# Routed experts of a transformer block: token rows and expert hidden values turned on TensorE in two fp16 parts instead of one fp32 transpose

## What is computed

```
logits = flat @ router_w
scores = softmax(logits)
_, topk_idx = top_k(logits + router_bias, 4)
topk_scores = scores[topk_idx] / sum(scores[topk_idx])
g = silu(einsum('nd,edf->nef', flat, wg))        # 64 experts, d = 512, f = 128
u = einsum('nd,edf->nef', flat, wu)
routed = einsum('ne,nef,efd->nd', comb, g * u, wd)
shared = einsum('nsh,shd->nd', silu(flat@swg) * (flat@swu), swd)
out = x + routed + shared
```

## Time and profile before

| | us |
|---|---|
| three runs: median, lowest, highest | 1222.91, 1222.49, 1225.0 |
| the profiled execution, its own time | 1227.31 |
| its span, from the first to the last instruction | 1225.5 |

### The profile page before, as it was taken

The page is one execution under the profiler, slowest core; times in us unless marked ns, Lnnn a source line. Parts: engine busy times, 40 slices in busy tenths (PEclk is TensorE's granted clock), DMA queues, the critical chain, the costliest instruction groups (busy, mean ns, idle before and its releaser), DMA issues.

```text
span 1225.5 us, 27577 instructions
## 1 busy us (share of the span) xinstructions
PE 1129.8 (92%) x9096; PEld 513.7 (42%) x9097; DVE 732.4 (60%) x1134; ACT 501.2 (41%) x944; POOL 422.1 (34%) x548
## 2 busy tenths in 40 slices
PE   6957899999999998999998999999999999997998
PEld 3523233333333333554444455544545454532443
DVE  6755899999999983877794123323323222335383
ACT  3311588889888897235211122222222222201010
POOL 5400134343343434015636323322333322145460
PEclk9979699999999999999999999999999999998999
DMA  8143232232312200521000588779886888665461
GB/s 241 66 129 110 41 81 41 53 65 40 77 40 52 65 21 21 187 105 34 1 1 16 168 298 283 249 246 327 264 269 184 279 293 286 189 165 175 151 178 63
DMA packets 75766, 169.98 MB, mean 139 GB/s; under 512 B 13764, under 2 KB 16324, under 8 KB 75716
## 3 DMA queue, kind: packets, MB, share of 16 engines
q1 hardware_dynamic: 45972, 100.59, 27.3%
q0 software_dynamic: 12800, 41.95, 11.8%
q10 hardware_dynamic: 16944, 26.75, 6.3%
HBM read 225.08 MB, written 41.42 MB: 217 GB/s over the span
## 4 chain that ended last, share of the span: by engine, by line
PE 65%; DVE 14%; issue 8%; DMA 6%; ACT 4%; POOL 1%; SPq 1%; DVEq 0%; ACTq 0%; POOLq 0%
PE PS L1320 13%; PE PS L1211 12%; PE PS L1336 7%; PE PS L1128 6%; PE PS L1293 6%; DVE maxes L1394 5%; PE PS L1307 4%; PE PS L1015 4%; PE PS L1181 3%; DVE max_low L1394 3%; DMA ring<-in_L_ffn_wg_dram 3%; PE PS L1106 3%; PE PS L1077 3%; ACT att L902 2%; PE PS L1328 2%
## 5 line engine op out<-in xcount | busy, mean ns | idle before, releaser
L902 ACT ACTIVATE att<-PS 128x512 f32<-128x512 f32 x576 | 312.6, 594 | 58.6 <-PE PS L1106 51.7
L1211 PE MATMUL PS<-XN,att 128*128 128x512 f16 x768 | 177.5, 392 | 16.2 <-issue 8.0
L1128 PE MATMUL PS<-att,v_head 128*32 128x256 f32 (+1 forms) x2560 | 178.6, 370 | 0.9 <-POOL att L717 0.9
L1394 DVE TENSOR_REDUCE maxes<-PS 128x2 f32<-128x1024 f32 (+2 forms) x192 | 172.8, 941 | 1.2 <-PE PS L1020 1.1
L1394 DVE TENSOR_REDUCE max_low<-PS 128x2 f32<-128x1024 f32 x128 | 153.7, 1210 | 20.5 <-PE PS L1015 18.1
L1015 PE MATMUL PS<-att 48*128 48x512 f16 (+7 forms) x768 | 117.9, 332 | 19.8 <-DMA att<-k_stacks 13.5
L1684 DVE TENSOR_TENSOR w_att<-w_att,PS 128x128 f32<-128x128 f32 x96 | 27.6, 288 | 168.6 <-issue 86.9
L966 ACT ACTIVATE w_att<-PS 128x512 f32<-128x512 f32 x96 | 57.2, 597 | 172.5 <-PE PS L1307 172.5
L1696 DVE COPY w_att<-PS 128x512 f32<-128x512 f32 x96 | 66.4, 692 | 101.1 <-DMA slot_y<-w_att 71.2
L1211 PEld LDWEIGHTS PS<-XN,att 128*128 128x128 f16 x768 | 76.3, 100 | 115.3 <-issue 23.6
L1106 PE MATMUL PS<-att 50*128 50x512 f16 (+1 forms) x640 | 112.0, 363 | 13.5 <-ACT att L902 11.1
(11 more groups left out here) (169 smaller groups left out, 1371.6 us busy)
## 6 DMA issues: line engine op xcount, KB each, us to landing
ring<-in_L_ffn_wg_dram SPq DMA_DIRECT2D x96, 512.0 KB
XT<-in_L_ffn_wg_dram SPq DMA_DIRECT2D x96, 512.0 KB
ring<-in_L_ffn_wd_dram SPq DMA_DIRECT2D x96, 256.0 KB
XT<-in_L_ffn_wd_dram SPq DMA_DIRECT2D x96, 256.0 KB
slot_y<-w_att ACTq DMA_DIRECT2D x192, 128.0 KB
att<-q_stacks SPq DMA_DIRECT2D x64, 192.0 KB, 3.9
q_stacks<-att SPq DMA_DIRECT2D x24, 256.0 KB
att<-k_stacks SPq DMA_DIRECT2D x64, 96.0 KB, 4.0
```

Source lines behind the costliest of these rows:

```text
L902: act.activation(probs[:, n0 % RING, u * BANK:(u + 1) * BANK], bank((2 * n0 + u) % EXP_BANKS), ACT.Exp, scale=HD ** -0.5 / QK_SCALE ** 2). ...
L1128: mm = pe.matmul(PS[32 * r:32 * r + 32, at:at + qn], v_head[b][:, kt, :], probs[:, (NS * b + s) % RING, a:a + qn], start=s in (0, NS0), st ...
L1211: mm = pe.matmul(bank(2 * (n % 2) + k), shared_w[:, 2 * k + w, C * s + c, at:at + P], v[:, c, tokens], start=(c == 0 and w == 0 and v is x ...
L1394: last = dve.reduce_max(out, src, AXX)
```

## The change

It does five things.

1. `turn_slots` on PE: the four fp32 transposes of a pair's tokens become eight fp16 matmuls against an fp16 identity, `xg_hi` and `xg_lo` added up in PSUM. In place of the gather's semaphore it waits for `xg_lo_done`.
2. The two parts are made in the loop: `tokens_high` on ACT (`xg` times 16, rounded to fp16), and `tokens_low` on DVE (the rest). Both read `xg` with a step of four elements and write without one. In body n they stand for pair n+2: on ACT behind `silu(n)`, on DVE behind `hidden_turned(n-1)`. Those of pairs 0 and 1 stand ahead of the loop. The scale is taken out again in `turned_tokens`.
3. The same for the hidden values: `e_high(n)` on ACT, `e_low(n)` on DVE, and two fp16 matmuls in `turn_hidden` in place of one fp32 transpose, the scale of 32 taken out in `hidden_turned`.
4. Gathers leave empty places out: the table holds token - 2048 for a filled slot, 2048 is added as it is copied, so an empty slot has index 2048, which the bounds check of the indirect DMA leaves out. POOL clears `xg` once ahead of the first gather. The gathers wait for `xg_lo_done` instead of `xg_turned`.
5. POOL makes the fp16 identity near the start of the program.

The new tiles `ht_hi` and `ht_lo` take the free end of `w_att`, `xg_hi` and `xg_lo` a part of `XT` behind the weights of lanes 4 to 7. The diff, without the declarations of the tile `ident_h` and of six semaphores:

```diff
--- before.py
+++ after.py
@@ -52,6 +52,7 @@
 
 
 X_SCALE, W_SCALE = 16.0, 64.0
+H_SCALE = 32.0
 XW = X_SCALE * W_SCALE
 QK_SCALE = 16.0
 
@@ -318,6 +320,8 @@
         lane_w += [carve(flat_xt, n * 3 * C * F, [P, 3, C * F])[0] for n in range(4)]
         xg, xgt, yb, sg, ht, hg = carve_all(w_att, 0, ([P, 4, D], FP32), ([P, 2, D], FP32), ([P, 2, D], FP32),
                                             ([P, 2, P], FP32), ([P, 2, P], FP32), ([P, 2, P], FP32))
+        ht_hi, ht_lo = carve_all(w_att, 4 * D + 2 * D + 2 * D + 6 * P, ([P, 2, P], F16), ([P, 2, P], F16))
+        xg_hi, xg_lo = carve_all(flat_xt, 4 * 3 * C * F, *[([P, 2, D], F16)] * 2)
         idx = sb("idx", [P, 4], U32)
 
         hot = [carve_all(arena, at, ([P, NT, 2 * PAIRS], F16), ([P, NT, SUB], F16))
@@ -641,6 +651,8 @@
                 pool.tensor_tensor(parts[n][2], parts[n][0], parts[n][1], ALU.subtract).then_inc(att_w_lo, 1)
 
             part_scale(0)
+            pool.wait_ge(ident_set, 1)
+            pool.tensor_copy(ident_h[:, :], ident[:, :]).then_inc(ident_h_set, 1)
             for b in range(BATCH):
                 pool.memset(v_head[b][:, :, :], 1 / X_SCALE).then_inc(v_ones, 1)
             pool.memset(mask_q[:, :], 0.0).then_inc(mask_zero, 1)
@@ -760,7 +772,8 @@
                 .then_inc(consts, 1)
             pool.tensor_copy(iota_c[:, :], idxf[:, 0:4, :].rearrange("p a b -> p (a b)").bitcast(U32))\
                 .then_inc(consts, 1)
-            pool.tensor_copy(token_f[:, :], token_f[:, :].bitcast(U32)).then_inc(consts, 1)
+            pool.tensor_scalar(token_f[:, :], token_f[:, :].bitcast(U32), float(-NTOK), None, ALU.add)\
+                .then_inc(consts, 1)
             pool.tensor_copy(iota_t[:, :, :], iota_t[:, :, :].bitcast(U32)).then_inc(consts, 1)
             pool.wait_ge(consts, 15)
 
@@ -820,15 +833,18 @@
             def gather_tokens(i, j):
                 n = JP * i + j
 
-                wait(pool, xg_turned, n - 3)
+                wait(pool, xg_lo_done, n - 3)
                 pool.tensor_copy(idx[:, j:j + 1], tab_t[:, bass.ds(j * LANE_TILES + i, 1)]).then_inc(idx_set, 1)
                 wait_alone(pool, idx_set, n + 1, pool_passed)
                 pool.indirect_dma_start(out=xg[:, j, :], out_offset=None, in_=xn2_rows[:, :],
-                                        in_offset=bass.IndirectOffsetOnAxis(ap=idx[:, j:j + 1], axis=0))\
+                                        in_offset=bass.IndirectOffsetOnAxis(ap=idx[:, j:j + 1], axis=0),
+                                        bounds_check=NTOK - 1, oob_is_err=False)\
                     .then_inc(xg_in[j], 16)
 
             pool.wait_ge(table_ready, 1)
             pool.wait_ge(xn2_stored, 16 * NT)
+            pool.memset(xg[:, :, :].rearrange("p n d -> p (n d)"), 0.0).then_inc(xg_zero, 1)
+            pool.wait_ge(xg_zero, 1)
             for j in range(JP):
                 gather_tokens(0, j)
             with pool.Fori(1, LANE_TILES) as i:
@@ -959,16 +975,29 @@
             for g in range(EARLY):
                 shared_silu(g)
 
+            def tokens_high(n, k, i):
+
+                act.wait_ge(xg_in[k % JP], 16 * (i + k // JP + 1))
+                wait(act, xg_turned, n - 1)
+                act.activation(xg_hi[:, k % 2, :].rearrange("p (c k) -> p c k", c=C),
+                               xg[:, k % JP, :].rearrange("p (k c) -> p c k", c=C), ACT.Copy, scale=X_SCALE)\
+                   .then_inc(xg_hi_done, 1)
+
             def turned_tokens(n, k):
                 act.wait_ge(xg_turned, n + 1)
 
                 wait(act, e_up, n - 1)
-                act.activation(xgt[:, k % 2, :], bank(k % 2), ACT.Copy).then_inc(xgt_ready, 1)
+                act.activation(xgt[:, k % 2, :], bank(k % 2), ACT.Copy, scale=1 / X_SCALE).then_inc(xgt_ready, 1)
 
             def silu(n, k):
                 act.wait_ge(e_up, n + 1)
                 wait(act, e_hidden, n - 1)
                 act.activation(sg[:, k % 2, :], bank(2 + k % 2, F), ACT.Silu).then_inc(e_silu, 1)
+
+            def e_high(n, k):
+
+                act.wait_ge(e_hidden, n + 1)
+                act.activation(ht_hi[:, k % 2, :], ht[:, k % 2, :], ACT.Copy, scale=H_SCALE).then_inc(e_hidden_hi, 1)
 
             def store_y(i, j):
                 act.wait_ge(yb_ready, JP * i + j + 1)
@@ -983,9 +1012,14 @@
                     if not (last and j == JP - 1):
                         turned_tokens(n + 1, j + 1)
                     silu(n, j)
+                    if not (last and j >= JP - 2):
+                        tokens_high(n + 2, j + 2, i)
+                    e_high(n, j)
                     if not (first and j < 3):
                         store_y(i if j == 3 else i - 1, (j + 1) % JP if j < 3 else 0)
 
+            for k in range(2):
+                tokens_high(k, k, 0)
             turned_tokens(0, 0)
             expert_pairs(0, True, False)
             with act.Fori(1, LANE_TILES - 1) as i:
@@ -1298,14 +1332,15 @@
             for g in range(EARLY):
                 shared(g)
 
-            def turn_slots(n, k, i):
-                j = k % JP
-                pe.wait_ge(xg_in[j], 16 * (i + k // JP + 1))
+            def turn_slots(n, k):
+                pe.wait_ge(xg_lo_done, n + 1)
 
                 wait(pe, xgt_ready, n - 1)
                 for c in range(C):
-                    mm = pe.transpose(PS[:, (k % 2) * BANK + c * P:(k % 2) * BANK + (c + 1) * P],
-                                      xg[:, j, c:D:C], ident[:, :])
+                    at = slice((k % 2) * BANK + c * P, (k % 2) * BANK + (c + 1) * P)
+                    part = slice(c * P, (c + 1) * P)
+                    pe.matmul(PS[:, at], xg_hi[:, k % 2, part], ident_h[:, :], start=True, stop=False)
+                    mm = pe.matmul(PS[:, at], xg_lo[:, k % 2, part], ident_h[:, :], start=False, stop=True)
                 mm.then_inc(xg_turned, 1)
 
             def expert_up(n, j, i):
@@ -1323,9 +1358,10 @@
                 mm.then_inc(e_up, 1)
 
             def turn_hidden(n, j):
-                pe.wait_ge(e_hidden, n + 1)
+                pe.wait_ge(e_hidden_lo, n + 1)
                 wait(pe, e_turned, n - 1)
-                pe.transpose(bank(6 + j % 2, P), ht[:, j % 2, :], ident[:, :]).then_inc(e_turn, 1)
+                pe.matmul(bank(6 + j % 2, P), ht_hi[:, j % 2, :], ident_h[:, :], start=True, stop=False)
+                pe.matmul(bank(6 + j % 2, P), ht_lo[:, j % 2, :], ident_h[:, :], start=False, stop=True).then_inc(e_turn, 1)
 
             def expert_down(n, j, i):
                 for l in range(2):
@@ -1342,7 +1378,7 @@
                 for j in range(JP):
                     n = JP * i + j
                     if not (last and j == JP - 1):
-                        turn_slots(n + 1, j + 1, i)
+                        turn_slots(n + 1, j + 1)
                     expert_up(n, j, i)
                     if not (first and j < 1):
                         turn_hidden(n - 1, (j - 1) % JP)
@@ -1351,7 +1387,8 @@
 
 
             pe.wait_ge(table_ready, 1)
-            turn_slots(0, 0, 0)
+            pe.wait_ge(ident_h_set, 1)
+            turn_slots(0, 0)
             expert_pairs(0, True, False)
             with pe.Fori(1, LANE_TILES - 1) as i:
                 expert_pairs(i, False, False)
@@ -1670,7 +1707,7 @@
                         hidden_low(n - 1)
                     if n == TABLE_AT + 1:
                         dve.wait_ge(table_done, 1)
-                        dve.tensor_copy(tab_t[:, :], bank(6, PAIRS)).then_inc(table_ready, 1)
+                        dve.tensor_scalar(tab_t[:, :], bank(6, PAIRS), float(NTOK), None, ALU.add).then_inc(table_ready, 1)
                 if g:
                     hidden_low(HC * (g + 1) - 1)
                 for t in range(4 * g, 4 * g + 4) if g else ():
@@ -1683,11 +1720,23 @@
                 at = (2 + j % 2) * BANK + F
                 dve.tensor_tensor(ht[:, j % 2, :], sg[:, j % 2, :], PS[:, at:at + F], ALU.mult).then_inc(e_hidden, 1)
 
+            def tokens_low(n, k):
+                dve.wait_ge(xg_hi_done, n + 1)
+                dve.scalar_tensor_tensor(out=xg_lo[:, k % 2, :].rearrange("p (c k) -> p c k", c=C),
+                                         in0=xg[:, k % JP, :].rearrange("p (k c) -> p c k", c=C), scalar=X_SCALE,
+                                         in1=xg_hi[:, k % 2, :].rearrange("p (c k) -> p c k", c=C), op0=ALU.mult,
+                                         op1=ALU.subtract).then_inc(xg_lo_done, 1)
+
+            def e_low(n, j):
+                dve.wait_ge(e_hidden_hi, n + 1)
+                dve.scalar_tensor_tensor(out=ht_lo[:, j % 2, :], in0=ht[:, j % 2, :], scalar=H_SCALE,
+                                         in1=ht_hi[:, j % 2, :], op0=ALU.mult, op1=ALU.subtract).then_inc(e_hidden_lo, 1)
+
             def hidden_turned(n, j):
                 dve.wait_ge(e_turn, n + 1)
 
                 wait(dve, e_down, n - 1)
-                dve.tensor_copy(hg[:, j % 2, :], bank(6 + j % 2, P)).then_inc(e_turned, 1)
```

(6 more changed lines are left out.)

7 lines of the change are left out of this document (added).

## The result

| | before | changed |
|---|---|---|
| median of four runs, us | 1222.7 | 1324.3 |
| lowest to highest, us | 1222.42 to 1225.0 | 1315.83 to 1327.32 |
| span of the profiled execution, us | 1225.5 | 1321.7 |

The ratio is 1.083, with a 95% interval of 1.078 to 1.088: about 101 us slower, outside the range of 1230 to 1305.

A forecast was written before the change was run, and what follows sets the result against it. The prediction took PE alone to bound the loop most of the time, at 3.83 us a pair. Terms 25.9 + 2 + 0.3 + 0.56 = +28.7 us on 1227.3 gave 1256.0, or 1251.6 against the median; range 1230 to 1305.

The forecast's parts named there:

- The closed chain: Routed loop: silu, both token conversions, token turn and up product follow one another, 4.23 us a pair, +25.9 us; chance 0.60.
- Where I chose: the step of four: Token conversions on ACT and DVE: reading xg with a step of 16 bytes was taken to cost nothing extra.
- the double price on both engines: Token conversions: time per element doubles on ACT and DVE, 92 us more, 1344 us; chance 0.07, left out of the range.
- the 2 us kept for late weights: Routed loop: waits for weights that remain despite the longer beat, 2 us, between 0 and 5.
- The other reading of the same rows: Weight load with the step: 0.07 us more for 128 elements, as a price per element 0.28 us on each engine.
- doublings: Token conversions at doubled time per element: 0.45 us more on ACT alone (1294 us), or also 0.53 on DVE (1344).
- PE's beat without waits: Routed loop: fp16 turns take 0.23 and 0.15 us off PE's beat of 3.83, leaving 3.45 us.
- The rows left out: Gathers in the loop: 4096 rows, 8.4 MB or 8% of bytes, moving the time by a microsecond or two at most.
- PE's idle time: Routed loop, before the token turn: PE stands idle some 0.7 us in every pair, released by DVE.
- The second: Rival for the loop: same chain, but the step of four costs time, 1294 to 1344 us; chance 0.27.
- The third: Rival for the loop: conversions run early enough, PE never waits, beat 3.45 us, total 1197 us; chance 0.05.
- The fifth: Rival for the loop: PE's idling lowers its clock; at half, products take twice as long, far above range; chance 0.04.

The follow-up runs named there:

- e1: Changed kernel with both token conversions reading and writing without a step, PE's weight loads taking the step instead; ratio to the kernel before 1.019.
- e2: Changed kernel, step kept, with tokens_high moved ahead of silu and tokens_low ahead of the hidden product; ratio to the kernel before 1.041.
- e3: Changed kernel with both the step removed from the conversions and their place moved ahead of silu and the hidden product; ratio to the kernel before 0.989.
- e7: Kernel before plus ten instructions behind its last work, reading 512 fp32 elements at steps 1 to 8; step 4 took 1.10 us on ACT, 1.06 on DVE.
- e6: Kernel before with only the hidden values split and turned by two fp16 products; ratio to the kernel before 0.998.
- e9: Changed kernel with empty slots holding index 0 again, so all 12,288 rows are fetched; ratio to the kernel before 1.082.
- e4: Kernel before with only the gathers' part: empty places left out by the bounds check, xg cleared once; ratio to the kernel before 0.991.
- e8: Changed kernel with conversions reading without a step but writing fp16 elements 256 bytes apart; 1768 us in its one run.
- e10: e3 with yb stores issued ahead of e_high and tokens_low of pairs 0 and 1 ahead of the last two shared additions; ratio to the kernel before 0.982.
- e12: e10 with empty slots holding index 0, so all 12,288 rows are fetched again; ratio to the kernel before 0.988.

## Why the prediction was wrong

**The mechanism held.** The closed chain from up product to up product through silu, `tokens_high`, `tokens_low` and the token turn is in the trace, link by link, with PE's wait released by DVE 94 times. e1, which takes the step away and leaves the place, has 4.14 us a beat where the sum said 4.23. e2 and e3 show that the place is what makes the chain.

**The step that failed is "Where I chose: the step of four".** I took nothing for it and gave the double price on both engines a chance of 0.07 and no place in the range. Measured, it is 0.51 us on ACT and 0.37 on DVE. The rest of the beat nearly cancels: 0.10 more for the eight products (0.55 and not 0.45), 0.11 less since ACT starts `tokens_high` 0.17 us after silu's start and not after its end, and 0.10 less between engines (0.04 + 0.04 + 0.06 and not 0.07 + 0.07 + 0.10). 4.23 + 0.51 + 0.37 + 0.10 - 0.11 - 0.10 = 5.00, as measured. Without the step the same sum gives 4.12, and e1 has 4.14. Over 94 beats 0.77 us more are 72 us, and with the slow first bodies the loop came out 76.9 us above the forecast 397.6, nearly the whole distance from 1252 to 1324; the 2 us kept for late weights weren't needed.

**What misled** was the earlier trace rows. That four weight loads with the step stand 0.12 us apart was read as a property of SBUF that holds for every engine. It holds for PE's loads: contiguous ones stand 0.12 us apart too (eight of L1190 in 1.01 us). The other reading of the same rows, 0.07 us more for 128 elements, gives 0.28 per 512 and was too low as well: e7 has 0.47 and 0.38. Where the Trainium skill ("SBUF — State Buffer", in its part on the DMA port swizzle) states a penalty and no row of the trace covers the engine in question, the price should have stood in the middle of the range and not at its rim. And two "doublings" were set apart from each other as if one engine might pay and the other not; they read the same memory with the same step.

**Smaller terms.** PE's beat without waits was put at 3.45 and is 3.67 (e3, e6): the fp16 products cost more beside fp32 ones. The rows left out were to be worth "a microsecond or two"; in the changed kernel they are worth nothing (e9), and in the kernel before 11 us (e4), because without them most of its late weights are gone. Late weights were rightly forecast to vanish in the changed kernel. The loop's start was missed: it costs some 3 us in long beats. PE's idle time was put at 0.7 us a beat and is 1.3: 0.88 more by the step, less 0.21 that the rest of the chain saved and 0.10 for PE's own dearer hidden turn. That the clock stays up held, except for the start. And 0.2% was too fine a measure: between sets of runs the median of the kernel before moved by 0.7%.

**The rivals.** The second was the right one, in its form with the double price on both engines (chance 0.07): 0.88 us a beat against its 0.98. The third (PE never waits) is nearly what e3 makes of the kernel, at a beat of 3.67 and not 3.45. The fifth, the clock, is what e8 shows.

## What to carry to other kernels

Before a value is made on one engine for another, write down what stands ahead of it in its engine's order and what that waits for: a conversion whose input was ready long ago can still close a ring through the consumer. When an engine's rows don't cover the access pattern of a new instruction, measure ten instances of it at a program's end, as in e7; a row of another engine is no price. And look for the part of a change that pays alone: here leaving 4096 rows out gives 11 us by itself, and the expensive part gains only once it is read without the step and stands ahead of silu and of the hidden product (e10 has 0.982 where the rows alone give 0.991, and e12, with all rows fetched, 0.988; e1 and e2, with one of the two edits each, are slower than the kernel before).

## What the runs showed of the hardware that was not expected

- Reading fp32 from SBUF on ACT or DVE: steps of 4 and 8 bytes are free (0.63 and 0.65 us per 512 elements on ACT), 12 bytes cost half (0.87), 16 and 32 bytes the whole (1.10, 1.11).
- Writing: fp16 with 8 bytes 1.28 to 1.31 us where packed takes 0.63 to 0.68; fp32 with 8 bytes 0.71 to 0.73; fp16 with 256 bytes 2.4 to 2.5 (e8 alone, where DVE's second input is read with that step too).
- A weight load of fp16 with 8 bytes between elements costs PE almost nothing (0.57 us for eight products against 0.55).
- Two fp16 products of 128 columns ahead of an fp32 one take 0.22 us (e6), though in a long run each takes 0.056; the last one takes 0.15.
- With PE waiting 1.3 us in a beat of 5 us the granted clock stayed at 1.00; with 3.8 us in a beat of 9.9 us (e8) it was 0.70 on average, and most up products took 3.6 us instead of 1.9, close to double.
